# Flamingo block on one core: later weight loads in SyncE's order, and two late weight pieces rounded behind the first key product

## The chip, the cores and the metric

One core of a Trainium2 chip runs the whole kernel. The metric is the device time of one execution in microseconds (us); the times below are medians over runs.

## The reference, cut to what matters

For 4 batches (B=4) of 512 tokens and 1024 context tokens, width 512, 16 heads of 32:

```python
x = x + tanh(g_xattn) * xattn(layernorm(x), ctx)
#   q = qdq(x) @ qdq(wq).T + bq ; k, v = split(ctx @ wkv.T + bkv)
#   o = softmax(q k.T / sqrt(32)) v ; out = qdq(o) @ qdq(wp).T + bp     (qdq: int8 fake quantisation)
x = x + tanh(g_ffn) * ffn(layernorm(x))
#   w' = w.astype(float8_e4m3fn) for gate_w, up_w (512 x 1536) and down_w (1536 x 512)
#   ffn = ((silu(x gate' * gs) * (x up' * us)) down') * ds
```

The three feed-forward weights must be rounded to fp8 values in the kernel. This rounding is the work that the change moves.

## The kernel before, in words

**Weight pieces.** The three weights are cut into 36 pieces of 128x512 (256 KB), numbered 0 to 35: gate 0 to 11, down tiles 6 to 11 are pieces 12 to 17, up 18 to 29, down tiles 0 to 5 are 30 to 35. Each piece takes three steps. SyncE (SP) loads it (`load_weights`, L528). VectorE (DVE) makes its magnitude in two instructions (`w_magnitudes`, L1179 and L1182), after the load and after the earlier user of the buffer is rounded. GpSimd (POOL) rounds it in two instructions (`round_weights`, L686 and L688; the second gives `w_done`). There are four buffers for pieces 0 to 27 (two in `acc`, two in `xres`), so the load of piece k waits on SP for the rounding of piece k-4; from piece 28 on there are two, both in `acc`, so it waits for piece k-2. Everything issued by SP runs in program order, so a load that waits holds back all behind it.

**Batch 0, attention.** 32 units follow each other, 8 for each of 4 head groups. A unit is 4 score products (L1540), 8 products with the values (L1557) and 8 row sums (L1571), with ScalarE (ACT) taking the exponentials (L877). Units 0 to 21 of batch 0 also carry the estimate of the row maxima: a difference product (L1445) and a maxima product (L1512) on TensorE (PE), a relu on ACT (L834) and a reduction on DVE (L1094). The maxima of a group are turned (L1467), written to `crow` by DVE (L1081), and sent by SP as one row into the stacked queries (`shift_row`, L552). The first scores of a group need the group's stacks (24 transfers of queries and keys, L542) and its row. Group 2 begins at unit 16 and group 3 at unit 24. For these two groups SP's order is: weight loads up to `W_AHEAD["stack g"]`, a wait for the last scores of the group that used the buffer, 12 transfers of queries and 12 of keys, with weight loads up to `W_STACK` behind each 4 of them, loads up to `W_AHEAD["shift g"]`, then the row.

**Batch 0, behind attention.** DVE normalises and quantises the attention output (L1261 to L989), and then in its order come `late_magnitudes(2)` (pieces 30, 31), the value tiles V1 to V3 of the next batch (L1186), `late_magnitudes(2)` (32, 33), V4, the four projection tiles (`PROJ`, L1287 and L1291), the moments, V5 and V6, the second normalisation (L1008, into `x2`), `late_magnitudes(2)` (34, 35), V7 and the low halves of x2 transposed (L1306). PE's order is `CHAIN`: transposes of the quantised output (OQT), V4, PROJ, V5 to V7, the next batch's x, transposes of x2 (X2T, L1373), which need all four L1008 done, then the query products and the eight key products K0 to K7 of the next batch. X2T2 takes V7's PSUM bank. In K2's middle PE runs the first difference product of the next batch (L1445), for which DVE must have done the low half of K0 (L1049), that of K1, and a key difference (L1067). Batches 1 and 2 run this same stage without late pieces. POOL's order is: rounding of pieces up to 29, the projection's bias into the residual, `W_CHAIN` = 4 pieces (30 to 33), the inverse deviation for x2 (L675), pieces 34 and 35.

Of the kernel before, what the change touches and what calls it, by code (L numbers as in the profile page):

```python
# [148 lines left out]
for _b in range(B):  # L149
    for _s in (STREAM0 if _b == 0 else STREAM):  # L150
# [28 lines left out]

W_EARLY, W_LATE = MT - len(EARLY_V), 6  # L180

W_CHAIN = 4
W_NONE = (3, 6, 9, 11, 13, 15, 17, 19)
W_UNITS = tuple(int(u not in W_NONE) for u in range(UNITS))
WP_UNITS, WP_ROWS = (0, 1, 3, 4, 6, 7, 9), (6, 9)
# [6 lines left out]
assert W_EARLY + sum(W_UNITS) + W_LATE == W_STEPS  # L192


W_AHEAD = {"keys1": 5, "shift0": 8, "queries1": 10, "shift1": 13, "stack2": 15, "shift2": 20, "stack3": 20,
           "shift3": 24, "residual": 30}
W_STACK = {2: (15, 16, 16, 16, 17, 17), 3: (20, 21, 21, 21, 21, 23)}
DOWN_FREE = 6
STACK_DMAS = 6 * HG + 1
X_COPIES = 1 + CT  # L200
# [10 lines left out]
def a_free_count(name):  # L211
    return sum(n[0] not in "SX" for n in A_SEQ0[:A_SEQ0.index(name) + 1])


def hi_count(b, name):
    return b * len(HI_SEQ) + (HI_SEQ0 if b == 0 else HI_SEQ).index(name) + 1
# [10 lines left out]
def d_full_count(b, name):  # L227
    return sum(map(len, D_SEQ[:b])) + D_SEQ[b].index(name) + 1


def d_free_count(b, name):
    return (sum(by_dve(n) for seq in D_SEQ[:b] for n in seq)
            + sum(map(by_dve, D_SEQ[b][:D_SEQ[b].index(name) + 1])))


def d_bank(b, name):
    return D_BANK[b][name]
# [9 lines left out]
def copies_count(b, name):  # L247
    return b * X_COPIES + TURNED.index(name) + 1
# [43 lines left out]
def exp_count(b, u, j):  # L292

    if single(b, u):
        return HG * u + j + 1
    return HG // 2 * (b * UNITS + u + SINGLES) + j // 2 + 1
# [24 lines left out]
def build(nc, ctxT, x, wq, wkvT, wp, gate_w, up_w, down_w, bqT, bkT, bv, bp, gsT, usT, ds,  # L321
          g_x, g_f, out):
    with ExitStack() as ctx:
# [131 lines left out]
        def bank(n, rows=P, dt=F32):  # L455
            v = ps[0:rows, n, :]
            return v if dt == F32 else v.bitcast(dt)
# [43 lines left out]
        def _(sp):  # L501
# [21 lines left out]
            def load_weights(upto):  # L523

                for k in range(loads[0], upto):
                    if W_BEFORE[k] is not None:
                        sp.wait_ge(w_done, W_BEFORE[k] + 1)
                    sp.dma_start(w_in[W_BUFFER[k]], w_steps[k][0]).then_inc(w_loaded[W_BUFFER[k]], 16)  # L528
                loads[0] = max(loads[0], upto)
# [9 lines left out]
            def stack(dst_of, sources, g, upto=(0, 0, 0)):  # L539
                for dst4, src in enumerate(sources):  # L540
                    for j in range(HG):
                        sp.dma_start(dst_of[dst4 * DH:(dst4 + 1) * DH, g % 2, j, :],  # L542
                                     src[j * DH:(j + 1) * DH, g, :]).then_inc(stack_in[g % 2], 16)
                    load_weights(upto[dst4])

            def shift_row(b, g):

                if b == 0:
                    sp.wait_ge(crow_ready, g + 1)
                else:  # L550
                    sp.wait_ge(d_free, d_free_count(b - 1, f"TOP{g}"))
                sp.dma_start(qst[96:97, g % 2, :, :], crow_rows(g)).then_inc(stack_in[g % 2], 16)  # L552
# [23 lines left out]
            stack(qst, (qhi, qlo, qhi), 0)  # L576
            load_weights(W_AHEAD["keys1"])
            sp.wait_ge(a_free, a_free_count("K3"))
            stack(kst, (khi, khi, klo), 1)
            load_weights(W_AHEAD["shift0"])  # L580
            shift_row(0, 0)
            sp.wait_ge(xq_ready, NT)
            load_x(1)
            sp.wait_ge(a_free, a_free_count("Q1"))
            stack(qst, (qhi, qlo, qhi), 1, (9, 9, W_AHEAD["queries1"]))
            load_weights(W_AHEAD["shift1"])
            shift_row(0, 1)

            for b in range(B):

                for g in range(2, G):
                    if b == 0:
                        load_weights(W_AHEAD[f"stack{g}"])
                    sp.wait_ge(s_full, exp_count(b, (g - 1) * MT - 1, HG - 1))
                    upto = W_STACK[g] if b == 0 else (0,) * 6
                    stack(qst, (qhi, qlo, qhi), g, upto[:3])
                    stack(kst, (khi, khi, klo), g, upto[3:])
                    if b == 0:
                        load_weights(W_AHEAD[f"shift{g}"])
                    shift_row(b, g)  # L600
# [39 lines left out]
        def _(pool):  # L640
# [41 lines left out]
            def round_weights(k):  # L682

                w, mag = w_in[W_BUFFER[k]], w_mag[W_BUFFER[k]]
                pool.wait_ge(w_magnitude, k + 1)
                nc.gpsimd.tensor_tensor(w, w, mag, ALU.add).then_inc(w_step, 1)  # L686
                pool.wait_ge(w_step, k + 1)
                nc.gpsimd.tensor_tensor(w_steps[k][1], w, mag, ALU.subtract).then_inc(w_done, 1)  # L688
# [19 lines left out]
            def first_units():  # L708
# [17 lines left out]
                pool.wait_ge(pe_setup, 3)  # L726
                for k in range(W_STEPS - W_LATE, W_STEPS - W_LATE + W_CHAIN):
                    round_weights(k)

            for b in range(B):  # L730
# [8 lines left out]
                if b == 0:  # L739
                    for k in range(W_STEPS - W_LATE + W_CHAIN, W_STEPS):  # L740
                        round_weights(k)
# [202 lines left out]
        def _(dve):  # L944
# [100 lines left out]
            def k_low(b, n, bank_no, free):  # L1045
                ct, half = divmod(n, 2)
                cols = slice(half * 512, (half + 1) * 512)
                dve.wait_ge(a_hi, hi_count(b, f"K{n}"))
                nc.vector.scalar_tensor_tensor(out=klo[:, ct, cols], in0=bank(bank_no),  # L1049
                                               scalar=bk_c[:, ct:ct + 1], in1=khi[:, ct, cols],  # L1050
                                               op0=ALU.add, op1=ALU.subtract).then_inc(free, 1)

            def q_scaled(n, src):

                nc.vector.scalar_tensor_tensor(
                    out=qt[:, n % 2, :], in0=src, scalar=sw_q[:, n:n + 1], in1=sx_bc,
                    op0=ALU.mult, op1=ALU.mult).then_inc(qt_ready, 1)

            def q_low(b, n, free):

                dve.wait_ge(a_hi, hi_count(b, f"Q{n}"))
                nc.vector.scalar_tensor_tensor(out=qlo[:, n, :], in0=qt[:, n % 2, :], scalar=bq_c[:, n:n + 1],
                                               in1=qhi[:, n, :], op0=ALU.add, op1=ALU.subtract).then_inc(free, 1)
# [104 lines left out]
            def w_magnitudes():  # L1168

                k = w_next[0]  # L1170
                if k == W_STEPS:
                    return
                w_next[0] += 1
                w, mag = w_in[W_BUFFER[k]], w_mag[W_BUFFER[k]]
                dve.wait_ge(w_loaded[W_BUFFER[k]], 16 * W_COUNT[k])
                if W_BEFORE[k] is not None:
                    dve.wait_ge(w_done, W_BEFORE[k] + 1)

                nc.vector.tensor_scalar(mag.bitcast(U16), w.bitcast(U16).rearrange("p (n h) -> p n h", h=2)[:, :, 1],  # L1179
                                        0x7F80, None, ALU.bitwise_and).then_inc(w_mask, 1)  # L1180
                dve.wait_ge(w_mask, k + 1)
                nc.vector.tensor_scalar(mag, mag, 2.0 ** -6, 1.5 * 2.0 ** 20, ALU.max, ALU.mult).then_inc(w_magnitude, 1)  # L1182
# [39 lines left out]
            for b in range(B):  # L1222
# [20 lines left out]
                def next_v(*tiles):  # L1243

                    for mt in tiles:
                        if not last:
                            v_tile(d_full, d_full_count(b, f"V{mt}"), d_bank(b, f"V{mt}"), d_free, mt)
# [21 lines left out]
                def late_magnitudes(n):  # L1269
                    for _ in range(n if b == 0 else 0):  # L1270
                        w_magnitudes()

                late_magnitudes(2)
                next_v(1, 2, 3)
                late_magnitudes(2)
                if last:
                    down_tile(b - 1, 1, b, "LATE1")

# [30 lines left out]
                def beside(name):  # L1309
                    for part in AHEAD[b].get(name, []):  # L1310
                        maxima(b + 1, part)

                if not last:
                    dve.wait_ge(x_copied, copies_count(b + 1, "SX"))
                    for n in range(CT):
                        name = f"Q{n}"
                        dve.wait_ge(d_full, d_full_count(b, name))
                        if n >= 2:
                            dve.wait_ge(d_free, d_free_count(b, f"Q{n - 2}"))
                        q_scaled(n, bank(d_bank(b, name)))  # L1320
                        if n >= 1:
                            q_low(b + 1, n - 1, d_free)
                    q_low(b + 1, CT - 1, d_free)
                    for n in range(8):
                        beside(f"K{n}")
                        k_low(b + 1, n, d_bank(b, f"K{n}"), d_free)

                for i in range(FT):
                    name = f"GU{2 * i + 1}"
# [454 lines left out]
```

## Time and profile before

| what | us |
| --- | --- |
| median of 3 runs | 920.49 (919.34 to 921.16) |
| profiled execution, device time | 921.14 |
| profiled execution, span of its instructions | 919.3 |
| PE busy | 856.7 (93%) |
| DVE busy | 674.4 (73%) |
| ACT busy | 554.2 (60%) |

The span is what the rows are placed in; the profiled execution's own time lies 1.84 us above its span and 0.65 us above the median. Rows give a start and a length in us from the span's start. A bracket behind a row is the idle time of that engine before it, and the work that ended the idle time. PE instructions overlap, so starts are compared with starts.

### The profile page before, as it was taken

To read this page: it belongs to the slowest core of one execution; us is meant where nothing else is said; L and a number is where in the kernel's file an instruction comes from. 1 tells how busy PE (TensorE), PEld (TensorE's weight loads), DVE (VectorE), ACT (ScalarE), POOL (GpSimd) and SP (SyncE) were. 2 spreads that over 40 slices of the span, in tenths; PEclk is the share of its full clock that TensorE was granted. 3 is DMA by queue.
4 is the path that set the end of the run, shared out by engine and by line. 5 is a ranking of instruction groups with operands and counts; after the bars stand their busy time and mean duration, and the time that the engine had idled before them with its cause. 6 is when DMAs were issued, how large, how long until landed. Compare 5 with 4: busy or idle time off the path is not lost.

```text
span 919.3 us, 13602 instructions
## 1 busy us (share of the span) xinstructions
PE 856.7 (93%) x4968; PEld 316.1 (34%) x4976; DVE 674.4 (73%) x1306; ACT 554.2 (60%) x737; POOL 249.3 (27%) x236
## 2 busy tenths in 40 slices
PE   5989989997999999999899999999999989998998
PEld 2422212244433332224443332224433322234444
DVE  6888956988676779968676678986867778788222
ACT  5547978752456559873456649884356779862230
POOL 1145755875127600001017700002002210020230
PEclk9999999999899999999999999999999999999899
DMA  9334333221201133200111133300010023200001
GB/s 331 105 87 133 95 112 91 75 89 46 52 24 47 44 124 98 52 1 1 26 50 35 42 112 99 78 2 1 9 44 1 1 61 102 53 1 30 5 1 46
DMA packets 37251, 55.29 MB, mean 60 GB/s; under 512 B 8960, under 2 KB 15424, under 8 KB 37184
## 3 DMA queue, kind: packets, MB, share of 16 engines
q1 hardware_dynamic: 35264, 48.13, 18.4%
q0 software_dynamic: 1920, 6.29, 2.3%
q8 instruction: 39, 0.64, 0.3%
q14 instruction: 28, 0.23, 0.1%
HBM read 31.21 MB, written 4.19 MB: 39 GB/s over the span
## 4 chain that ended last, share of the span: by engine, by line
PE 66%; DVE 16%; issue 8%; ACT 7%; DMA 1%; POOL 1%; SPq 0%; ACTq 0%; DVEq 0%; POOLq 0%
PE ps L1389 32%; PE ps L1577 8%; PE ps L1540 7%; PE ps L1557 7%; DVE acc L1119 4%; ACT r L877 4%; PE ps L1512 4%; PE ps L1571 3%; PE ps L1585 1%; PE ps L1373 1%; DVE kst L1094 1%; DVE am L974 1%; DVE r L1261 1%; DVE vv L1186 1%; DVE xq L1094 1%
## 5 line engine op out<-in xcount | busy, mean ns | idle before, releaser
L877 ACT ACTIVATE r<-ps 128x1024 f32<-128x1024 f32 (+1 forms) x300 | 253.3, 901 | 59.6 <-PE ps L1540 57.2
L1094 DVE CUSTOM_DVE_ANT_0 kst<-ps,kst 128x512 f32<-128x512 f32 x192 | 124.5, 685 | 30.3 <-PE ps L1512 28.4
L1540 PE MATMUL ps<-qst,kst 97*128 97x512 f16 x512 | 138.7, 385 | 7.4 <-DMA qst<-crow 4.7
L1557 PE MATMUL ps<-r,vv 128*32 128x512 f32 x1024 | 138.1, 612 | 3.3 <-ACT r L877 3.2
L1119 DVE TENSOR_TENSOR acc<-acc,r 128x1024 f32<-128x1024 f32 x120 | 138.6, 1216 | 0.0
L834 ACT ACTIVATE kst<-ps 128x1024 f32<-128x1024 f32 x96 | 98.2, 1023 | 53.3 <-PE ps L1445 53.0
L1389 PE MATMUL ps<-xs,w_gate 128*128 128x512 f16 x384 | 92.6, 385 | 1.5 <-DVE xs L1306 1.5
L1389 PE MATMUL ps<-xs,w_up 128*128 128x512 f16 x384 | 91.2, 380 | 0.0
L1540 PEld LDWEIGHTS ps<-qst,kst 97*128 97x128 f16 x512 | 40.4, 97 | 145.0 <-ACT r L877 86.7
L932 ACT ACTIVATE qst<-ps,gs_c 128x512 f32<-128x512 f32 x48 | 33.0, 688 | 69.4 <-PE ps L1389 69.4
L1335 DVE SCALAR_TENSOR_TENSOR xq<-ps,us_c,qst 128x512 f32<-128x512 f32 x48 | 36.0, 749 | 52.3 <-PE ps L1389 52.3
L1577 PE MATMUL ps<-w_down,r 128*128 128x512 f16 (+1 forms) x312 | 66.2, 363 | 0.0
L750 POOL TENSOR_TENSOR r<-xq,r 128x512 f16<-128x512 f32 x36 | 42.6, 1184 | 72.3 <-ACT r L925 71.9
L1389 PE MATMUL ps<-ctx_hi,wkv_hi 128*128 128x512 f16 x128 | 49.1, 388 | 13.9 <-ACT ctx_hi L770 10.9
L1512 PE MATMUL ps<-k_reg,q_reg 32*128 32x512 f16 x256 | 49.6, 384 | 6.5 <-DVE mx L1094 5.9
L1445 PE MATMUL ps<-acc,q_reg 32*128 32x512 f16 x256 | 49.6, 384 | 3.9 <-issue 2.8
L1389 PEld LDWEIGHTS ps<-xs,w_gate 128*128 128x128 f16 x384 | 35.9, 99 | 47.7 <-issue 6.9
L1389 PEld LDWEIGHTS ps<-xs,w_up 128*128 128x128 f16 x384 | 34.7, 98 | 45.3 <-issue 8.7
L700 POOL TENSOR_TENSOR xres<-xres,bp_bc 128x512 f32<-128x512 f32 x12 | 14.9, 1273 | 129.3 <-ACT r L885 128.5
L1389 PE MATMUL ps<-ctx_lo,wkv_hi 128*128 128x512 f16 x128 | 48.9, 387 | 0.3 <-DVE ctx_lo L1129 0.3
L1389 PE MATMUL ps<-ctx_hi,wkv_lo 128*128 128x512 f16 x128 | 48.6, 384 | 0.0
L1389 PE MATMUL ps<-wkv_lo,ctx_hi 128*128 128x512 f16 x128 | 48.6, 379 | 0.0
(166 smaller groups left out, 1286.1 us busy)
## 6 DMA issues: line engine op xcount, KB each, us to landing
kst<-k_reg SPq DMA_DIRECT2D x192, 64.0 KB
qst<-q_reg SPq DMA_DIRECT2D x192, 32.0 KB
xs<-in_x SPq DMA_DIRECT2D x4, 1024.0 KB, 5.9
cf<-in_ctxT POOLq DMA_DIRECT2D x16, 256.0 KB, 3.5
xres<-in_x SPq DMA_DIRECT2D x3, 1024.0 KB, 5.1
out<-xres SPq DMA_DIRECT2D x12, 256.0 KB, 2.0
acc<-in_down_w SPq DMA_DIRECT2D x10, 256.0 KB, 2.7
vv<-in_wkvT SPq DMA_DIRECT2D x2, 1024.0 KB, 9.8
```

The lines of the kernel that those rows point to most:

```text
L750: nc.gpsimd.tensor_tensor(f2_at(b, 1, i), fus[:, i % 2, :], f2_at(b, 0, i), ALU.subtract).then_inc(f_ready, 1)
L834: nc.scalar.activation(kept(b, n), ps[:, first_bank:first_bank + 2, :], ACT.Relu, scale=2.0).then_inc(diff_kept, 1)
L877: nc.scalar.activation(prob[:, s:s + heads, :], ps[:, first_bank:first_bank + heads, :], ACT.Exp, scale=SCALE).then_inc(exp_done, 1)
L1094: ins = nc.vector.tensor_tensor_reduce(kept(b, n)[:, k, :], bank(PAIR + k), kept(b, n)[:, k, :], 1.0, -3.0e38, ALU.add, ALU.max, mx[:, g % ...
L1119: nc.vector.tensor_tensor(sums, other, prob[:, p:p + ADD_HEADS, :], ALU.add).then_inc(p_dve, 1)
L1335: nc.vector.scalar_tensor_tensor(out=fus[:, i % 2, :], in0=bank(d_bank(b, name)), scalar=us_c[:, i:i + 1], in1=tmp[:, i % 2, :], op0=ALU.m ...
L1389: mm = nc.tensor.matmul(out, l, r, start=(k == 0), stop=(k == len(terms) - 1))
L1445: mm = nc.tensor.matmul(bank(first_bank + k), qhi[rows, g, i // 2 * P:(i // 2 + 1) * P], kdiff[rows, g % 2, :], start=True, stop=True)
L1512: mm = nc.tensor.matmul(bank(PAIR + k), qhi[rows, g, t * P:(t + 1) * P], khi[rows, g, 512:1024], start=True, stop=True)
L1540: mm = nc.tensor.matmul(bank(first_bank + k), kst[0:97, g % 2, j + k, t * P:(t + 1) * P], qst[0:97, g % 2, j + k, :], start=True, stop=True)
L1557: mm = nc.tensor.matmul(ps[j * DH:(j + 1) * DH, O_BANK, :], vv[:, t, h * DH:(h + 1) * DH], prob[:, p_slot(b, u, j), :], start=(t == 0), st ...
L1577: mm = nc.tensor.matmul(out[:, cols], f2_at(b, part, i)[:, t * P:(t + 1) * P], w_down[:, i, cols], start=(i == 0 and part == 0), stop=(i = ...
```

## The change

SP's order of weight loads in groups 2 and 3 of batch 0 is altered, and the two pieces 32 and 33 on DVE go behind the normalisation of x2, where 34 and 35 were, and 34 and 35 go behind the low half of K0. On POOL pieces 32 and 33 go behind the inverse deviation.

```diff
-W_CHAIN = 4
+W_CHAIN = 2
...
-W_AHEAD = {"keys1": 5, "shift0": 8, "queries1": 10, "shift1": 13, "stack2": 15, "shift2": 20, "stack3": 20,
-           "shift3": 24, "residual": 30}
-W_STACK = {2: (15, 16, 16, 16, 17, 17), 3: (20, 21, 21, 21, 21, 23)}
+W_AHEAD = {"keys1": 5, "shift0": 8, "queries1": 10, "shift1": 13, "stack2": 15, "shift2": 17, "stack3": 19,
+           "shift3": 23, "residual": 30}
+W_STACK = {2: (15, 15, 15, 15, 15, 16), 3: (19, 19, 19, 20, 20, 22)}
...
                 late_magnitudes(2)
                 next_v(1, 2, 3)
-                late_magnitudes(2)
                 if last:
                     down_tile(b - 1, 1, b, "LATE1")
...
                     for n in range(8):
                         beside(f"K{n}")
                         k_low(b + 1, n, d_bank(b, f"K{n}"), d_free)
+                        late_magnitudes(2 * (n == 0))
```

A number n in `W_AHEAD` or `W_STACK` means that pieces up to n-1 are loaded at that place. So before, pieces 17, 18 and 19 stood ahead of group 2's row, and piece 23 was the last ahead of group 3's row; in the changed kernel these are piece 16 and piece 22.

## Rows read from the trace of the kernel before

**Rows 1.** The page: the span, and the chain that ended last, by engine
```profile
span 919.3 us, 13602 instructions
...
PE 66%; DVE 16%; issue 8%; ACT 7%; DMA 1%; POOL 1%; SPq 0%; ACTq 0%; DVEq 0%; POOLq 0%
```

**Rows 2.** Waits of PE: us in total, times, longest
```profile
PE ps L1373 <- DVE r L1008: 6.8, 2, 4.3
...
PE ps L1540 <- DMA qst<-crow: 4.7, 2, 3.9
```

**Rows 3.** The chain of waits in time, batch 0, 131 to 136 us
```profile
131.55 1.17 POOL w_down L688
...
133.10 2.33 DMA qst<-crow
```

**Rows 4.** Timeline of PE, units 15 to 18 of batch 0
```profile
131.22 0.39 PE L1445 MATMUL ps<-acc,q_reg 32*128 32x512 f16 x2
135.48 1.03 PE L1540 MATMUL ps<-qst,kst 97*128 97x512 f16 x2 [3.87 <-DMA qst<-crow]
...
140.12 0.39 PE L1445 MATMUL ps<-acc,q_reg 32*128 32x512 f16 x2
...
143.51 0.39 PE L1445 MATMUL ps<-acc,q_reg 32*128 32x512 f16 x2
```

**Rows 5.** Timeline of SP's queue, around the rows of groups 2 and 3
```profile
125.52 7.54 SPq L528 DMA_DIRECT2D xres<-in_up_w  x2
...
162.37 0.64 SPq L552 DMA_DIRECT2D qst<-crow  x1
```

**Rows 6.** Timeline of POOL, rounding of piece 18
```profile
157.65 1.16 POOL L688 TENSOR_TENSOR w_up<-xres 128x512 f16<-128x512 f32 x1
```

**Rows 7.** Timeline of DVE, the rows of maxima and the end of attention
```profile
126.96 0.68 DVE L1081 TENSOR_SCALAR crow<-ps 4x512 f16<-4x512 f32 x1
...
160.14 0.68 DVE L1081 TENSOR_SCALAR crow<-ps 4x512 f16<-4x512 f32 x1 [0.65 <-PE ps L1467]
...
194.56 0.69 DVE L1186 TENSOR_TENSOR vv<-ps,bv_bc 128x512 f32<-128x512 f32 x1 [3.57 <-PE ps L1389]
```

**Rows 8.** Windows: busy us of each engine, PE's granted clock, DMA share, GB/s
```profile
136.00:140.00 4.00, 4.00 (x20) 0.49 (x18) 0.00 (x0) 3.04 (x6) 0.00 (x0) 0.64 0.40 117
...
229.00:232.00 3.00, 2.16 (x9) 1.99 (x11) 2.37 (x4) 0.97 (x2) 2.92 (x3) 0.50 0.02 5
...
446.00:450.00 4.00, 2.49 (x13) 0.94 (x12) 3.77 (x6) 1.88 (x3) 0.00 (x0) 1.00 0.03 7
```

**Rows 9.** Timeline of PE behind attention of batch 0: OQT, X2T2, difference in K2
```profile
206.01 1.05 PE L1373 MATMUL ps<-identb,r 128*128 128x128 bf16 x16 [1.53 <-ACT r L900]
...
229.62 1.97 PE L1373 MATMUL ps<-identf,r 128*128 128x128 f32 x8 [1.35 <-DVE vv L1186]
...
243.92 0.39 PE L1445 MATMUL ps<-acc,q_reg 32*128 32x512 f16 x2 [0.92 <-issue]
```

**Rows 10.** Timeline of DVE in the same stage of batch 0
```profile
210.59 0.43 DVE L1179 TENSOR_SCALAR acc<-acc 128x512 uint16<-128x512 uint16 x1 [1.99 <-DMA acc<-in_down_w]
...
212.84 1.25 DVE L1179 TENSOR_SCALAR acc<-acc 128x512 uint16<-128x512 uint16 x1 [1.50 <-DMA acc<-in_down_w]
...
226.72 0.42 DVE L1179 TENSOR_SCALAR acc<-acc 128x512 uint16<-128x512 uint16 x1
...
228.88 0.68 DVE L1186 TENSOR_TENSOR vv<-ps,bv_bc 128x512 f32<-128x512 f32 x1
...
242.46 0.75 DVE L1049 SCALAR_TENSOR_TENSOR k_reg<-ps,bk_c,k_reg 128x512 f16<-128x512 f32 x1 [1.65 <-ACT k_reg L795]
```

**Rows 11.** Timeline of PE in the same stage of batch 1: OQT, K0, difference in K2
```profile
425.07 1.05 PE L1373 MATMUL ps<-identb,r 128*128 128x128 bf16 x16 [1.12 <-ACT r L900]
...
448.67 0.39 PE L1389 MATMUL ps<-ctx_hi,wkv_hi 128*128 128x512 f16 x1 [1.51 <-DVE q_reg L1062]
...
456.24 0.39 PE L1445 MATMUL ps<-acc,q_reg 32*128 32x512 f16 x2 [0.92 <-issue]
```

## The prediction

> **What bounds the kernel now.** I read the chain that ended last first: two thirds of it is PE, and no DMA engine or POOL matters as a whole [rows 1]. So a change is worth what it takes from PE's idle time or gives PE in clock, and only where PE really waits. The list of PE's waits then says which places the change can touch. Two of its entries belong to them: scores that waited for the row `qst<-crow`, 4.7 us in two waits, the longest 3.9, and transposes L1373 that waited for DVE's normalisation L1008, longest 4.3 [rows 2]. The reader is to see next that each of these costs more than its idle time. In the timeline of PE the step from one difference product to the next is 143.51 - 140.12 = 3.39 us in an undisturbed unit, and 140.12 - 131.22 = 8.90 us across the first wait [rows 4]. That is 5.51 us lost, of which 3.87 is idle. The rest is clock: in the window 136 to 140 us the granted clock is 0.64 of full [rows 8], so PE ran partly at 1.2 GHz instead of 2.4 after it had stood still. The same is seen after the other wait: 0.50 at 229 to 232 us [rows 8].
>
> **Part one, the rows of maxima.** The row of group 2 was issued at 133.10 and took 2.33 us; what stood before it was the rounding of piece 15, which ended at 131.55 + 1.17 = 132.7 [rows 3], because the load of piece 19 waits for it on SP and stands ahead of the row. The two loads 18 and 19 held SP from 125.52 for 7.54 us [rows 5]. The maxima themselves were in `crow` at 126.96 + 0.68 = 127.64 [rows 7]. In the changed kernel only pieces 15 and 16 are loaded between the stacks and the row, and they need the roundings of 11 and 12, which are past. SP then waits for `crow` alone: issued at 127.7, landed at 127.7 + 2.4 = 130.1. PE wants it when the product that began at 131.22 has ended, at 131.6 [rows 4]. There are 1.5 us to spare, so the whole 5.5 us goes.
>
> Moved past this row are the loads of 17, 18 and 19. Pieces 17 and 18 follow right behind it, by about 129; piece 18 was loaded after 125.52 before and rounded at 157.65 [rows 5, 6], so a few us don't matter. Piece 19 goes behind 16 transfers of group 3 at 0.64 us each (the length of one issue in [rows 5]), to about 141; DVE wants it next after piece 18, 3 us or so behind, at some 153 by the new times. Pieces 20 to 22 move behind more of group 3's stack, whose transfers in return are not held by them. The loads that leave the front of the row cost SP the same issue time behind it, where SP next waits for TensorE anyway.
>
> The row of group 3 was issued at 162.37 [rows 5], though `crow` was written at 160.14 + 0.68 = 160.82 [rows 7]. What stood ahead was piece 23, which waits for the rounding of 19. In the changed kernel the last one ahead is piece 22, which waits for piece 18: done at 157.65 + 1.16 = 158.8 [rows 6], two us before the maxima. The row comes 1.5 us earlier, and the second wait, 4.7 - 3.9 = 0.8 to 0.9 us [rows 2], goes. Part one is 5.5 + 0.9 = 6.4 us.
>
> What could take it back is DVE. Behind the second row it has work without a gap until it waits 3.57 us for PE's first value tile at 194.56 [rows 7]. It starts earlier by 5.5 and PE arrives earlier by 6.4, so 2.7 us of that wait are left: DVE doesn't become the bound. Should it, the cost is what PE gained past 3.57 us, at the very most 6.4 - 3.57 = 2.8. Below nothing I see no row: part one is between 3.6 and 6.4, and I take 6.4, since every wait in it hangs on PE's pace.
>
> **Part two, pieces 32 and 33.** DVE waited 1.99 and 1.50 us for their loads, ahead of V4 and the projection [rows 10]. The two loads wait for the roundings of 30 and 31, so this wait is built in. Batches 1 and 2 run the same stage without late pieces, and so give its price whole. From the transposes of the quantised output to the difference product in K2, batch 0 takes 243.92 - 206.01 = 37.91 us [rows 9] and batch 1 takes 456.24 - 425.07 = 31.17 us [rows 11]. The difference is 6.74 us, and it holds 4.3 of idle [rows 2], the 1.35 before X2T2 [rows 9] and the half clock.
>
> Three pairs of magnitudes remain in the changed kernel. The pair 30 and 31 lies where it did, beside PE's value tiles, in both kernels: nothing. The pair 32 and 33 takes the place of 34 and 35 behind the normalisation, 228.88 - 226.72 = 2.16 us ahead of V7 [rows 10]. It still holds back X2T2 by some 1.5 us, but in batch 1 what follows is not bound by PE: K0 waits 1.51 us for DVE's query work [rows 11], which itself waits for ACT's copies of x and x2. I take 0.3 us for it; bounds 0 and 2.16. The pair 34 and 35 is new behind K0's low half. There DVE waits 1.65 us for ACT's half of K1 [rows 10]; 2.16 - 1.65 = 0.5 us is left over, and it is on the path, for PE already waits 0.92 us for the key difference [rows 9]. After it DVE has time again in each key product (PE needs 12 products for it). Bounds: 0.5 as worked out and 2.16 if the cover were gone. Their loads must be there too: 35's waits for the rounding of 33. POOL needs four instructions of 1.16 us [rows 6] for the two, so it is done about 5.5 us behind the normalisation and the data some 3 us later, at 8.5; K0's low half ends 14 us behind the normalisation before (226.72 to 242.46 - 1.65 [rows 10]) and about 12 in the changed kernel. Margin 3.5 us. POOL's own next work is at K7, five key products later. The queries' stack for batch 1, behind these loads on SP, waits for the low half of Q0 and that is later still: nothing.
>
> Part two is 6.74 - 0.3 - 0.5 = 5.9 us; bounds by the worst of each, 6.74 - 2.16 - 2.16 = 2.4, and 6.74 - 0.5 = 6.2.
>
> **What the clock does to it.** Of the 5.9 us, 4.3 is idle time and 1.6 is mostly clock. In batch 1 PE idles 1.12, 1.51 and 0.92 us in this stage [rows 11] and keeps 1.00 in the window that holds the 1.51 [rows 8]; it was 0.50 only behind the wait of 4.3. So I expect full clock with the 1.5 us that remain before X2T2. The Trainium skill, in TensorE: Matmul & The Clock Gate, section "A second HAM failure mode: psum-queue depth-cycling", speaks against it: TensorE that idles briefly but often between groups of matmuls swings between the two clock levels. By that rule the stage would keep its low clock, and the gain would be 1.6 us less; batch 1's window does not bear it out.
>
> **Sum.** 6.4 + 5.9 = 12.3 us. The profiled execution has 919.3 of span and 1.84 around it, 921.14. Less 12.3 it is 908.8, and 0.65 less for the median of the runs shown: 908.2 us. All that follows hangs on PE in the same order, so the gain is carried to the end.
>
> **The rivals.**
> *A, forecast:* 908.2; its own range 906.5 to 910. Chance 0.60.
> *B, the low clock stays behind X2T:* the short idle before X2T2 is enough. For it: the clock was 0.50 there [rows 8] and this idle stays. Against it: batch 1. 908.2 + 1.6 = 909.8. Chance 0.15.
> *C, DVE becomes the bound in one of the two stages:* the unbroken work up to 194.56 gives back up to 2.8 us, or the pair behind K0 costs its whole 2.16 instead of 0.5. For it: the gaps are small, 3.57 and 1.65 [rows 7, 10]. Against it: both were counted. 908.2 + 1.7 to 2.8 = 910 to 911. Chance 0.13.
> *D, more than forecast:* short waits of PE that come from the same queues also shrink, or the pair behind the normalisation is wholly hidden. 905 to 906.5. Chance 0.07.
> *E, no change:* the row lands as late as before, because another transfer or the stack itself, not the load of 19, holds it, and PE's wait before X2T only moves behind K0. Against it: the chain names the rounding of piece 15 ahead of the row [rows 3]. 920.5 less little, 919 to 921. Chance 0.02.
> *F, slower:* the load of piece 35 comes late and DVE stands behind K0 with the key difference, and PE with it. Its margin is 3.5 us and the sum's gain 12.3, so it decides only if the load lands 16 us or more late; 2 us beyond that gives 922.5. For it: DVE is in order, and a wait there holds PE one to one. Against it: no load here is that late. Chance 0.03.
>
> Less than 0.2% (1.8 us) is about what a measurement of this kernel can't tell from no change. Faster is A to D, 0.95; the same 0.02; slower 0.03. The range from 905.5 to 911.5 takes in A, B, most of C and D: about 0.9, and I keep it that wide because the terms of B and C can add up.
>
> **What the changed profile would show.** PE's wait for `qst<-crow` in batch 0 gone from both places, and a step of 3.39 us between difference products at units 16 and 17, with a granted clock of 1.00. SP's row of group 2 within 0.2 us of the end of `crow`. DVE without a wait for `acc<-in_down_w` ahead of V4, and the transposes X2T starting right behind those of x. The stage from OQT to K2's difference product 32 us long. PE's wait there about 1.4 us instead of 0.92. Wrong would be the prediction if the idle before X2T2 grew past 1.5 us, if the low clock were there in both kernels, or if DVE waited for a load of pieces 19 to 23, 34 or 35.

## The result and the profile after

The changed kernel takes 909.82 us (median of 4 runs, 908.40 to 911.38), the kernel before 920.83 us in the same comparison (919.34 to 921.73). The ratio is 0.9882, with a 95% interval of 0.9861 to 0.9903: 11.0 us faster between the medians. The forecast was 908.2, 12.3 us faster, with a range from 905.5 to 911.5. The profiled execution of the changed kernel took 909.84 us. Below, a time "on the path" is the time between two starts of PE inside one profiled execution.

The page of the changed kernel, which answers to [rows 1]: the span, and the chain that ended last.

```profile
span 908.0 us, 13602 instructions
...
PE 67%; DVE 16%; ACT 8%; issue 8%; DMA 1%; ACTq 0%; DVEq 0%
```

The waits of PE after, which answer to [rows 2]. The wait for `qst<-crow` is not in the list any more, and of the two waits for L1008 the one of 4.3 us is gone. Two entries hold a longer wait than before: L1373 waits for L900 up to 2.1 us (1.5 before), and L1445 waits up to 1.8 us ("issue") where it was 0.92 [rows 9]. The wait of 2.5 us is in the last batch, as before.

```profile
PE ps L1373 <- ACT r L900: 4.4, 3, 2.1
PE ps L1445 <- issue: 3.6, 3, 1.8
...
PE ps L1373 <- DVE r L1008: 2.5, 1, 2.5
```

SP's queue after, around the two rows; it answers to [rows 3, 5]. The row of group 2 is issued at 126.95, when DVE has just written `crow` (126.24 + 0.68 = 126.92); one load of piece 17 and one of 18 follow, and piece 19 stands in the middle of group 3's stack at 140.56.

```profile
126.95 0.64 SPq L552 DMA_DIRECT2D qst<-crow  x1
127.64 0.44 SPq L528 DMA_DIRECT2D acc<-in_down_w  x1
128.12 0.43 SPq L528 DMA_DIRECT2D xres<-in_up_w  x1
...
140.56 0.58 SPq L528 DMA_DIRECT2D xres<-in_up_w  x1
...
154.80 0.64 SPq L552 DMA_DIRECT2D qst<-crow  x1
```

PE's timeline after: the difference products that answer to [rows 4], and the stage behind attention that answers to [rows 9].

```profile
130.51 0.39 PE L1445 MATMUL ps<-acc,q_reg 32*128 32x512 f16 x2
133.91 0.39 PE L1445 MATMUL ps<-acc,q_reg 32*128 32x512 f16 x2
...
137.46 0.39 PE L1445 MATMUL ps<-acc,q_reg 32*128 32x512 f16 x2
...
199.64 1.05 PE L1373 MATMUL ps<-identb,r 128*128 128x128 bf16 x16 [2.15 <-ACT r L900]
...
216.13 1.04 PE L1373 MATMUL ps<-identf,r 128*128 128x128 f32 x8
218.70 1.09 PE L1373 MATMUL ps<-identf,r 128*128 128x128 f32 x8 [1.53 <-DVE vv L1186]
...
231.96 0.39 PE L1445 MATMUL ps<-acc,q_reg 32*128 32x512 f16 x2 [1.76 <-issue]
...
236.51 0.49 PE L1512 MATMUL ps<-k_reg,q_reg 32*128 32x512 f16 x2
```

The product at 130.51 is the one that began at 131.22 before, so the step across group 2's start is 133.91 - 130.51 = 3.40 us instead of 8.90, as the prediction had it. The step behind it is 137.46 - 133.91 = 3.55 us, where it was 3.39; this 0.16 us is not explained here. Both steps together take 6.95 us instead of 12.29. The transposes X2T begin at 216.13 without a wait, and the second half of them waits 1.53 us (1.35 before). DVE doesn't wait for a load of pieces 19 to 23 or 30 to 35; from 120 us on its only wait for a weight piece is 0.16 us, at 182.59. The stage from OQT to the difference in K2 takes 231.96 - 199.64 = 32.32 us instead of 37.91.

DVE after, around the places where it took longer than I had counted, and the wait that answers to [rows 7].

```profile
187.57 0.69 DVE L1186 TENSOR_TENSOR vv<-ps,bv_bc 128x512 f32<-128x512 f32 x1 [2.67 <-PE ps L1389]
...
193.82 1.20 DVE L978 TENSOR_SCALAR sx<-am 128x4 f32<-128x4 f32 x1
...
228.44 0.29 DVE L1182 TENSOR_SCALAR acc<-acc 128x512 bf16<-128x512 bf16 x1
...
229.10 1.12 DVE L1182 TENSOR_SCALAR acc<-acc 128x512 bf16<-128x512 bf16 x1
230.14 0.74 DVE L1049 SCALAR_TENSOR_TENSOR k_reg<-ps,bk_c,k_reg 128x512 f16<-128x512 f32 x1
230.81 1.05 DVE L1067 CUSTOM_DVE_ANT_0 acc<-k_reg 128x512 f16<-128x512 f16 x1
```

L978 took 0.58 us in the kernel before and 1.20 now; L1067, the key difference, 0.68 before and 1.05 now. L1182, the second instruction of a magnitude, took 0.29 us for piece 34 and 1.12 for piece 35. The three long ones run beside POOL work. POOL after:

```profile
190.05 4.95 POOL L700 TENSOR_TENSOR xres<-xres,bp_bc 128x512 f32<-128x512 f32 x4 [0.53 <-DMA xres<-in_x]
...
228.81 1.27 POOL L686 TENSOR_TENSOR acc<-acc 128x512 f32<-128x512 f32 x1 [7.33 <-DVE acc L1182]
230.15 1.15 POOL L688 TENSOR_TENSOR w_down<-acc 128x512 f16<-128x512 f32 x1
231.26 1.60 POOL L686 TENSOR_TENSOR acc<-acc 128x512 f32<-128x512 f32 x1
```

L978 begins at 193.82 inside the bias additions and ends with them at 195.0. Before, it also ended with them (200.80 + 0.58 = 201.38 against 196.41 + 4.95 = 201.36). The second L1182 begins when POOL has just started on piece 34, and L1067 runs while POOL rounds pieces 34 and 35.

**A budget of the profiled executions.** A start near 99 us, ahead of the change, serves as zero (L1512 at 99.81 before and at 99.10 after; all work up to there is the same, and its 0.7 us are not the change's). From there to the difference in K2 it is 243.92 - 99.81 = 144.11 us before and 231.96 - 99.10 = 132.86 after: 11.25 us gained. The parts: 12.29 - 6.95 = 5.34 at group 2, 0.93 at group 3 (from batch 0's last difference product to L1501, 171.00 - 153.70 = 17.30 us before and 164.02 - 147.65 = 16.37 after), less 0.61 from L1501 to OQT, where L978 grew by 0.62, and 37.91 - 32.32 = 5.59 in the stage behind OQT, which sum to 11.25. From there to the last batch's OQT 1.6 us is lost, 1.5 of it to the clock in K2, and behind that 0.95 is regained, through the clock again; both are told below. With the 0.7 us at the front this gives the 11.3 us between the two profiled executions, and without it 10.6 us.

### The profile page after: what moved, and what is told of

It reads as the page before. It is cut to its first block, busy times and chain, and to the rows that moved or that the text cites. A ratio compares the mean times of both kernels' runs of the same rounds, so it can differ in the third digit from the quotient of the medians.

```text
span 908.0 us, 13602 instructions
## 1 busy us (share of the span) xinstructions
PE 852.6 (94%) x4968; PEld 315.4 (35%) x4976; DVE 674.8 (74%) x1306; ACT 553.6 (61%) x737; POOL 249.0 (27%) x236
## 4 chain that ended last, share of the span: by engine, by line
PE 67%; DVE 16%; ACT 8%; issue 8%; DMA 1%; ACTq 0%; DVEq 0%
PE ps L1389 33%; PE ps L1577 9%; PE ps L1540 7%; PE ps L1557 7%; ACT r L877 4%; DVE acc L1119 4%; PE ps L1512 4%; PE ps L1571 3%; PE ps L1585 1%; PE ps L1373 1%; DVE kst L1094 1%; DVE am L974 1%; DVE r L1261 1%; ACT r L900 1%; DVE vv L1186 1%
## 5 line engine op out<-in xcount | busy, mean ns | idle before, releaser
L1512 PE MATMUL ps<-k_reg,q_reg 32*128 32x512 f16 x256 | 50.0, 387 | 6.5 <-DVE mx L1094 5.9
L1445 PE MATMUL ps<-acc,q_reg 32*128 32x512 f16 x256 | 50.0, 386 | 4.7 <-issue 3.6
L675 POOL TENSOR_TENSOR rstd<-mv,mhalf 128x4 f32<-128x4 f32 x8 | 9.9, 1240 | 141.8 <-DVE mv L1005 141.8
```

The lines of the kernel that those rows point to most:

```text
L1445: mm = nc.tensor.matmul(bank(first_bank + k), qhi[rows, g, i // 2 * P:(i // 2 + 1) * P], kdiff[rows, g % 2, :], start=True, stop=True)
L1512: mm = nc.tensor.matmul(bank(PAIR + k), qhi[rows, g, t * P:(t + 1) * P], khi[rows, g, 512:1024], start=True, stop=True)
```

## The experiments

Each is compared with runs of the kernel before that were made beside it. **Theory 1:** each part removes its own wait of PE, the parts add up, and what is short of the forecast is DVE work that takes longer beside POOL and a clock fall behind PE's wait for the key difference. **The rivals** were that DVE becomes the bound and gives time back, that the low clock has nothing to do with the waits, and, for single steps, those in the expectations.

**One part alone.** Both sets of numbers in SP's order, and nothing else:

```diff
-... "stack2": 15, "shift2": 20, "stack3": 20, "shift3": 24, ...
-W_STACK = {2: (15, 16, 16, 16, 17, 17), 3: (20, 21, 21, 21, 21, 23)}
+... "stack2": 15, "shift2": 17, "stack3": 19, "shift3": 23, ...
+W_STACK = {2: (15, 15, 15, 15, 15, 16), 3: (19, 19, 19, 20, 20, 22)}
```

> SyncE's new order of loads alone, late pieces 32 to 35 where they were. Theory 1 (each part removes its own wait of TensorE and they add up): both waits for the row of maxima are gone, 5.4 us at group 2 and 0.9 at group 3, and up to 0.6 comes back where DVE's small scale operation (L978) waits for GpSimd's bias additions, so 5.7 to 6.3 us below the kernel before, about 914.8. The wait of 4.3 us ahead of the transposes of x2 and the low clock behind it are still there. Rival (the time is given back later because DVE, without a gap in this stage, becomes the bound): 2.8 us or more less than that, 917.5 or above, and DVE's 3.57 us wait for the first value tile is gone.

Measured: 915.56 us, ratio 0.9935 (0.9920 to 0.9949), 5.2 us below the median of the kernel before beside it, 920.76; the ratio says 6.0 us, with an interval from 4.7 to 7.4. In its trace the wait for `qst<-crow` is gone, and L978 took 1.28 us. From the L1512 near 100 us to OQT it takes 201.12 - 100.51 = 100.61 us, against 206.01 - 99.81 = 106.20 before and 199.64 - 99.10 = 100.54 in the changed kernel. Part one is 5.6 us on the path. The expectation was 5.7 to 6.3 us; the medians give just less than that and the ratio lies inside. The rival, 3.5 us or less, falls: the interval begins at 4.7, and DVE still waits 2.66 us for the first value tile. In one point the expectation missed. PE's wait ahead of the transposes of x2 is 2.43 us here and not 4.3, because the clock had already fallen behind the wait of 2.23 us ahead of OQT and PE came later; the stage still takes 238.60 - 201.12 = 37.48 us, for X2T waits for DVE in any case.

**The other part alone.** The late pieces moved, `W_CHAIN = 2`, SP's order as before:

```diff
                 late_magnitudes(2)
                 next_v(1, 2, 3)
-                late_magnitudes(2)
...
+                        late_magnitudes(2 * (n == 0))
```

> Only the late pieces moved, SyncE's loads as before. Theory 1: the stage from the transposes of the quantised output to the difference product in K2 takes 32.3 us as in the changed kernel instead of 37.9, a gain of 5.6, of which 1.5 is lost again if the clock falls behind the longer wait for the key difference: 4.1 to 5.6 us below before, 915 to 916.5. Rival (the low clock behind the 4.3 us wait was luck of the execution): 4.3 less 0.8 at most, 3.5 us or less.

Measured: 915.45 us, ratio 0.9943 (0.9929 to 0.9956), 5.3 us below. PE's timeline in this kernel:

```profile
206.33 1.05 PE L1373 MATMUL ps<-identb,r 128*128 128x128 bf16 x16 [1.55 <-ACT r L900]
...
238.66 0.39 PE L1445 MATMUL ps<-acc,q_reg 32*128 32x512 f16 x2 [1.75 <-issue]
...
243.36 0.39 PE L1512 MATMUL ps<-k_reg,q_reg 32*128 32x512 f16 x2
```

The stage takes 238.66 - 206.33 = 32.33 us, the 32.32 of the changed kernel, and the time lies in the expected 915 to 916.5, so the rival of 3.5 us or less falls. The parts add up: 5.59 us up to OQT in the first kernel and 37.91 - 32.33 = 5.58 behind it in this one make 11.17, against 11.25 with both. The product of the two ratios is 0.9878, the changed kernel's is 0.9882.

This trace also prices the wait for group 2's row a second time. It is 3.88 us here and 3.87 in the kernel before, yet the two steps across it take 13.50 us and not 12.29: the granted clock was 0.50 from 134 to 140 us, where in the kernel before it was back to 0.78 from 138 us.

**What held the row back.** The changed kernel with two of the three loads ahead of the row again, and then with all three:

```diff
-"shift2": 17, "stack3": 19
+"shift2": 19, "stack3": 19
```

```diff
-"shift2": 17, "stack3": 19
+"shift2": 20, "stack3": 20
```

> The changed kernel with the loads of pieces 17 and 18 ahead of group 2's row again, and only piece 19 behind it. Theory 1 (the row was late because the load of piece 19 waits for the rounding of piece 15; an issued load itself costs nothing): piece 18 needs the rounding of 14, which ends 2 us before the maxima are there, so the row goes out with the maxima and the time is that of the changed kernel, within 0.5 us. Rival (the loads themselves, 256 KB each on the same queue, hold the row back): the row lands 0.7 to 2.5 us later than in the changed kernel, and TensorE waits for what goes beyond its 1.5 us of margin, up to 1 us, with the low clock behind it up to 2.5.

> The changed kernel with the loads of pieces 17, 18 and 19 ahead of group 2's row again, all else as changed. Theory 1: the 3.9 us wait and the low clock behind it come back, 5.4 us over the changed kernel, 915 us; the wait at group 3 stays away. Rival (with the loads in the stacks moved, SyncE runs earlier and hides it): less than 3 us over.

Measured: with two loads ahead 909.95 us, ratio 0.9880 (0.9866 to 0.9893), which is the changed kernel's. The wait for the row is absent, and the row is issued at 127.69, when `crow` is written (126.98 + 0.68 = 127.66): the two loads did not hold it at all. With all three 915.07 us, ratio 0.9933 (0.9919 to 0.9946), 5 us more, near the expected 5.4. The chain of waits in the second kernel:

```profile
130.34 1.17 POOL w_down L688
...
131.52 0.33 SPq L528
...
131.89 2.21 DMA qst<-crow
...
134.15 1.04 PE ps L1540 x2
```

POOL's rounding of piece 15, the load of 19, the row, the scores: the link is the one that [rows 3] showed. One load more in front of the row turns nothing into 5 us, because that load waits and the two others don't. That an issued load of 256 KB holds the row back is ruled out for these two. On the path this kernel loses 6.4 us (237.89 - 98.61 = 139.28 against 132.86), again with the clock at 0.50 from 134 to 140 us behind the wait.

**The row of group 3.** Its one load put back:

```diff
-"shift3": 23
+"shift3": 24
```

> The changed kernel with the load of piece 23 ahead of group 3's row again, all else as changed. Theory 1: TensorE's wait of 0.8 us for the row comes back, and DVE then reaches L978 later against GpSimd's bias additions, so that L978 falls from 1.2 us to 0.6: 0.3 us over the changed kernel, which the times can't tell from none, but which the traces show as the span from the second maxima row to the transposes of the quantised output. Rival (the two are not bound to each other): L978 stays at 1.2 us and it is 0.9 us slower.

Measured: 909.44 us, ratio 0.9870 (0.9851 to 0.9889), no difference to the changed kernel that the times can tell. In its trace PE waits again and L978 is shorter:

```profile
158.50 1.04 PE L1540 MATMUL ps<-qst,kst 97*128 97x512 f16 x4 [0.75 <-DMA qst<-crow]
...
199.60 1.05 PE L1373 MATMUL ps<-identb,r 128*128 128x128 bf16 x16 [1.41 <-ACT r L900]
```

```profile
194.51 0.46 DVE L978 TENSOR_SCALAR sx<-am 128x4 f32<-128x4 f32 x1
```

From the L1512 near 99 (98.97 here) to OQT it takes 100.63 us, 100.54 with the load behind the row. POOL's bias additions begin 190.05 - 99.10 = 90.95 us behind the L1512 in the changed kernel and 189.99 - 98.97 = 91.02 here, but L978 begins at 94.72 and 95.54. So removing the wait of 0.8 us at group 3 brought DVE forward and not POOL, and L978 met the additions earlier: 0.9 gained, 0.7 to 0.8 given back, 0.09 us on the path where 0.3 was expected. The rival falls.

**The key difference and the clock behind it.** The changed kernel with pieces 34 and 35 one behind K4 and one behind K5:

```diff
-                        late_magnitudes(2 * (n == 0))
+                        late_magnitudes(int(n in (4, 5)))
```

> The changed kernel with pieces 34 and 35 one behind K4's low half and one behind K5's, instead of both behind K0's. Theory 1 (the missing 1.3 us of the forecast is the key difference, late by 0.84 us, and the low clock that follows TensorE's wait of 1.76 us there): that wait is back to 0.9 us, the clock stays at full through K2, DVE takes each piece in its slack of 0.8 us per key product, and the kernel is 0.8 to 2.4 us faster than the changed one. Rival (that clock fall is luck of the execution and not bound to this wait): 0.8 us or less. Second rival (DVE's slack does not hold them): TensorE waits for the maxima behind K5 and K6, same time or slower than the changed kernel.

Measured: 908.25 us, ratio 0.9869 (0.9854 to 0.9885). PE in this kernel, and L1067:

```profile
200.73 1.59 PE L1373 MATMUL ps<-identb,r 128*128 128x128 bf16 x16 [2.08 <-ACT r L900]
...
233.89 0.39 PE L1445 MATMUL ps<-acc,q_reg 32*128 32x512 f16 x2 [0.92 <-issue]
...
236.91 0.39 PE L1512 MATMUL ps<-k_reg,q_reg 32*128 32x512 f16 x2
```

```profile
233.10 0.68 DVE L1067 CUSTOM_DVE_ANT_0 acc<-k_reg 128x512 f16<-128x512 f16 x1
```

The wait is 0.92 again and L1067 0.68 us, so the pair's place cost 0.84 us. Some 0.5 of it came because K1's low half began at 230.14 in the changed kernel, and ACT's half of K1 was there at 228.95 + 0.69 = 229.64; 0.37 came because L1067 took longer. The first part too belongs to the work beside POOL: with 0.29 us instead of 1.12 for the second L1182, the pair would have ended at 229.10 + 0.29 = 229.39, ahead of ACT (an estimate from these rows). In this kernel, with one piece at a time, both L1182 take 0.29 us, and POOL is idle while they run. The same long second L1182 is in the 2.16 us of a pair in [rows 10]. K2's second half takes 236.91 - 233.89 = 3.02 us; in the changed kernel it was 236.51 - 231.96 = 4.55. But the time gained is 1.6 us between medians with overlapping intervals, so it doesn't decide between 0.8 and 2.4. The second rival falls, as the time is no longer than the changed kernel's.

The kernel with two loads ahead of the row decides more. It has the same wait of 1.76 us, and there K2's second half takes 237.39 - 234.37 = 3.02 us. The windows of the changed kernel, and then those of that one (the third number from the end is the granted clock):

```profile
233.00:236.00 3.00, 3.00 (x10) 1.02 (x8) 0.75 (x1) 1.10 (x2) 1.09 (x1) 0.56 0.45 105
```

```profile
200.00:204.00 4.00, 3.62 (x21) 2.35 (x22) 2.93 (x5) 2.28 (x5) 3.84 (x4) 0.57 0.15 35
233.00:236.00 3.00, 1.63 (x9) 0.73 (x10) 1.27 (x3) 1.02 (x1) 2.92 (x3) 1.00 0.30 70
```

In one execution the clock fell behind the wait of 1.76 us in K2, in the other it did not, and fell instead behind the wait of 2.15 us ahead of OQT. In the stage from OQT to K2 of all twelve traces, the clock fell behind the wait of 1.75 to 1.76 us in K2 in four executions of five, and behind the wait of 2.08 to 2.24 us ahead of OQT in three of six. It fell behind the two longer waits too (2.43 and 4.29 us ahead of X2T), not behind one of 1.86 us ahead of K0, and no fall began behind a wait of 1.60 us or less. So the low clock was seen to begin only behind the longer waits, and which of them it follows differs from one execution to the next; what decides it is not shown.

**V7 and the pair 32 and 33.** In the kernel with the pair 34 and 35 behind K4 and K5, the two lines exchanged:

```diff
-                late_magnitudes(2)
                 next_v(7)
+                late_magnitudes(2)
```

> As the kernel with pieces 34 and 35 behind K4 and K5, and V7's addition ahead of the pair 32 and 33 instead of behind it. Theory 1 (the pair's cost there is covered by DVE's query work, the price taken was 0.3 us): TensorE's wait of 1.5 us ahead of X2T2 goes and nearly all of it comes back as the wait of K0 for DVE's query work, so the stage from the transposes of the quantised output to the difference in K2 changes by 0.5 us at most. Rival (the 1.5 us are on the path): the stage is 1.5 us shorter. Second rival: DVE does the same work in another order and its low halves of x2 still wait, so nothing changes at all.

Measured: 907.77 us, ratio 0.9861 (0.9841 to 0.9880). PE in this kernel:

```profile
199.93 1.05 PE L1373 MATMUL ps<-identb,r 128*128 128x128 bf16 x16 [2.24 <-ACT r L900]
...
223.59 0.39 PE L1389 MATMUL ps<-ctx_hi,wkv_hi 128*128 128x512 f16 x1 [1.57 <-DVE q_reg L1062]
231.16 0.39 PE L1445 MATMUL ps<-acc,q_reg 32*128 32x512 f16 x2 [0.92 <-issue]
```

All 16 transposes X2T run in one piece from 216.41, without the 1.5 us wait ahead of X2T2, and K0 waits 1.57 us instead of 0.31. The stage takes 31.23 us. The same stage without this exchange, at full clock, is 230.94 - 199.45 = 31.49 us (the kernel below). So the exchange gives 0.26 us, and not the pair's 2.16 or PE's 1.5; against the 31.17 of batch 1, which has no late pieces, the pair cost 0.32 us where it stood. The rival falls, and so does the second one, for the wait did move to K0. The time is within the noise of the kernel without the exchange.

**What stretched L978.** POOL's bias additions of batch 0 left out, on the kernel with the pair behind K4 and K5:

```diff
-                residual_bias(0)
...
-                dve.wait_ge(x_biased, b * NT + NT)
+                if b == 0:
+                    dve.wait_ge(x_in, 16)
+                else:
+                    dve.wait_ge(x_biased, (b - 1) * NT + NT)
```

> As the kernel with pieces 34 and 35 behind K4 and K5, and without GpSimd's addition of the projection's bias to the residual in batch 0; that part of the computation is left out. Theory 1 (DVE's small scale operation L978 takes 1.1 to 1.3 us instead of 0.2 because GpSimd's addition runs beside it): it takes 0.15 to 0.2 us, TensorE's wait ahead of the transposes of the quantised output falls from 2.1 to 1.1 us, and the kernel is about 1.0 us faster, up to 1.7 where the clock had fallen behind the longer wait. Rival (L978 waits for its own inputs, the last reduction): L978 stays at 1 us or more and the time doesn't move.

Measured: 906.58 us, ratio 0.9843 (0.9830 to 0.9856). DVE, then PE, in this kernel (its line numbers are shifted by one or two, so L977 is L978 of the others, L1375 is L1373 and L1447 is L1445):

```profile
194.65 0.17 DVE L977 TENSOR_SCALAR sx<-am 128x4 f32<-128x4 f32 x1
```

```profile
199.45 1.05 PE L1375 MATMUL ps<-identb,r 128*128 128x128 bf16 x16 [1.12 <-ACT r L899]
...
230.94 0.39 PE L1447 MATMUL ps<-acc,q_reg 32*128 32x512 f16 x2 [0.92 <-issue]
```

Without POOL beside it the operation takes 0.17 us, and PE's wait falls to 1.12. That is a whole microsecond for an instruction on four columns. The rival, that L978 waits for its own inputs, falls: it has the same inputs here. The median is 1.7 us below that of the kernel with the additions, but from another comparison; the trace's 1.0 us is the closer price.

**A kernel that keeps the bias.** Again with the pair 34 and 35 behind K4 and K5, and the additions in halves, the second half behind the rounding of 31:

```diff
-                residual_bias(0)
+                residual_bias(0, range(2))
...
                 for k in range(W_STEPS - W_LATE, W_STEPS - W_LATE + W_CHAIN):
                     round_weights(k)
+                residual_bias(0, range(2, NT))
...
                     if t >= 2:
+                        dve.wait_ge(x_biased, b * NT + NT)
```

> As the kernel with pieces 34 and 35 behind K4 and K5, and GpSimd adds the bias to two tiles of batch 0's residual where it did and to the other two behind the rounding of 30 and 31; DVE waits for those ahead of its third projection tile. Theory 1: L978 takes 0.15 to 0.2 us, TensorE waits 1.1 us ahead of the transposes instead of 2.1, 1.0 us gained; the two late additions end some 0.5 to 1 us before DVE wants them, but run beside DVE's additions with two operands from SBUF, which may lengthen two of those by 0.3 to 0.5 us each: net 0 to 1 us faster. Rival (late additions are late): DVE waits ahead of the third projection tile and the kernel is no faster.

Measured: 908.94 us, ratio 0.9859 (0.9845 to 0.9872), inconclusive as a time. In the trace L978 is 0.17 us, PE waits 1.12 us ahead of OQT, and one of the additions beside POOL is longer (L1292 of DVE, 0.69 us in the other three tiles):

```profile
206.74 0.98 DVE L1292 TENSOR_TENSOR xres<-xres,qst 128x512 f32<-128x512 f32 x1
```

The stage takes 231.81 - 200.03 = 31.78 us instead of 31.49, so 0.3 of the 1.0 us is given back, as expected.

**All three.** Pair behind K4 and K5, V7 first, bias in halves:

> The three improvements together: pieces 34 and 35 behind K4 and K5, V7 ahead of the pair 32 and 33, bias in halves. Theory 1: the gains add up in TensorE's path, from the 32.3 us of the changed kernel to some 31.5 us for the stage from the transposes of the quantised output to the difference in K2 (0.84 for the key difference, 0.26 for V7, 0.3 lost to the lengthened addition), and 1.0 us earlier at its start; with no wait over 1.6 us there the clock stays at full in the stage. 907 us or a little less, 2 to 3 us below the changed kernel. Rival: they hide one another, and it is within 0.5 us of the best of them alone.

Measured: 906.42 us, ratio 0.9846 (0.9828 to 0.9865), the fastest complete kernel here. PE in it:

```profile
198.62 1.05 PE L1375 MATMUL ps<-identb,r 128*128 128x128 bf16 x16 [1.12 <-ACT r L901]
...
230.16 0.39 PE L1447 MATMUL ps<-acc,q_reg 32*128 32x512 f16 x2 [0.92 <-issue]
```

From its L1512 at 99.12 to this difference it is 131.04 us, against 132.86 in the changed kernel: 1.82 us on the path. The single gains, 0.84 for the key difference, 0.26 for V7 and 1.0 less 0.3 for the bias, make 1.80, so they add up and the rival falls; V7 and the bias were not tried each without the pair's new place. K2's second half takes 3.02 us here and 4.55 in the changed kernel, for the clock. The medians differ by 3.4 us between two comparisons, with intervals that overlap; 1.8 is what is shown.

## Why the prediction was right, and where its sum was off

**What bounds, and where.** Right. PE's two groups of waits were the places, and both went, but for 1.53 us ahead of X2T2, which the forecast had left there at about 1.5. The time of 909.82 us is also, to the figure, that of rival B, 909.8; this is chance, for B's low clock behind X2T did not come, and the granted clock was 1.00 there.

**Group 2's row.** Forecast 5.5 us. The step across the wait gave 5.50, of which 0.16 was lost in the next step: 5.34 in the traces, and by putting the loads back alone, 5 us in the times. Cause shown by the pair of kernels with two and with three loads ahead: the wait inside the load of piece 19. That the figure came out so near is in part luck, for it holds the low clock behind the wait as one execution had it; in two others the same two steps took 13.4 and 13.5 us and not 12.29.

**Group 3's row.** The wait of 0.9 us went away as forecast (0.93 measured), and the forecast's step "every wait in it hangs on PE's pace" failed there. POOL's bias additions hang on the residual's load, which did not come earlier with this wait; DVE came 0.6 us nearer to them, and L978 grew from 0.58 to 1.20. I had checked that DVE has idle time left (2.67 us, forecast 2.7), and not what POOL does beside it.

**The late pieces.** Forecast 5.9 us from the comparison with batch 1, measured 5.59. The pair behind the normalisation was priced at 0.3 and is 0.26 to 0.32. The pair behind K0 was priced at 0.5, as 2.16 us of work under a cover of 1.65, and is 0.84. Both the second L1182 and L1067 took longer while POOL rounded the very pieces that the pair hands over; the 2.16 us held one such long L1182 already, and L1067's 0.37 was left out. By the estimate above, the pair would have been covered without POOL beside it. That is the mis-sized term of part two.

**The clock.** I expected full clock behind the idle time ahead of X2T2, and so it was in the changed kernel. What I left out is the place behind it: the longer wait for the key difference was in the forecast (1.4 us, measured 1.76), and a fall behind it was not. The clock fell to 0.56 there in one trace and stayed at 1.00 in another. The Trainium skill (TensorE: Matmul & The Clock Gate, "A second HAM failure mode: psum-queue depth-cycling") tells of idle times between groups of matmuls that are short but frequent. The traces agree with it only in that the clock swings: in this stage it fell behind single waits of 1.75 us and more, in some executions, and no fall began behind a wait of 1.60 us or less.

**The sum.** 12.3 forecast; 11.25 on the path up to K2: short by 0.62 for L978, 0.34 for the pair behind K0 and 0.16 at group 2, with 0.07 over in the other terms. The medians give 11.0. The clock in K2 takes 1.5 us of the profiled execution, and the last batch gives 0.95 of it back, which is luck as well: from its OQT (832.21 before, 821.86 after) to the end of the span it takes 87.1 us before and 86.1 after. In both the clock fell there behind the wait of 2.55 us for L1008, but in the kernel before the low stretch reached into the gate products. PE's first gate products before, and then after:

```profile
852.18 3.57 PE L1389 MATMUL ps<-xs,w_gate 128*128 128x512 f16 x8 [1.49 <-DVE xs L1306]
```

```profile
842.62 1.89 PE L1389 MATMUL ps<-xs,w_gate 128*128 128x512 f16 x8 [1.49 <-DVE xs L1305]
```

So a single pair of profiles can be a microsecond or two off for the clock alone, and where a stage's price is wanted it is better read between two marks inside it. Behind the same wait of 2.55 us no fall is to be seen in two of the twelve traces. One execution of each kernel was traced, so how often the clock falls in any one kernel stays open.

## What to carry to other kernels

In a queue that runs in order, ask of each transfer ahead of an urgent one whether it waits, not how large it is: two loads in front of the row cost nothing and a third cost 5 us, because only the third waited for a rounding. A stage that other batches run without the extra work gives the price of that work whole, clock and covers included, and was good to 0.3 us here. When an engine is brought forward, look also at what the engines beside it do at that time: VectorE operations that took longer beside GpSimd gave back 0.6 and 0.8 us of 12.

## What the runs showed of the hardware

A VectorE instruction on 128x4 values took 0.17 us alone (L978, the traces without the bias additions beside it), and 0.46 to 1.29 us when it began inside a run of GpSimd additions; in each of the nine traces with the four additions together it ended within 0.1 us of the end of the last one. A bf16 operation of 128x512 that stays in SBUF (L1182) took 0.29 us with GpSimd idle and 1.12 to 1.14 us in every late pair, where the second one begins 0.2 to 0.3 us behind the start of a GpSimd rounding; that GpSimd is the cause is read from this meeting in time, and from the single late pieces, which all took 0.29. An operation of 128x512 with both operands from SBUF went from 0.68 to 1.05 us (L1067) and from 0.69 to 0.98 us (L1292) beside GpSimd, though another L1292 beside the same additions kept its 0.69. In the stage of the change, TensorE's granted clock fell behind seven of twelve waits of 1.75 to 2.24 us, at the same places and with the same lengths as where it didn't, behind both longer ones (2.43 and 4.29 us), and no fall began behind a wait of 1.60 us or less.
